# One program per engine for feed-forward and experts, with a first table for four expert pieces

## The reference, cut to what matters

```python
gate_logits = x_flat @ gate_w.T
topk_vals, topk_idx = jax.lax.top_k(gate_logits, K)
topk_w = jax.nn.softmax(topk_vals, axis=-1)
comb = comb.at[jnp.arange(T)[:, None], topk_idx].add(topk_w)
for e in range(E):
    h = jax.nn.gelu(x_flat @ w1[e].T + b1[e], approximate=False)
    y = h @ w2[e].T + b2[e]
    out = out + comb[:, e:e + 1] * y
```

## Time and profile before

| what | value |
|---|---|
| median of 3 runs | 1071.52 us (1066.3 to 1072.51) |
| profiled execution, its own time | 1073.44 us |
| its span in the trace | 1071.7 us |
| PE busy in the span | 948.8 us (89%) |
| DVE, ACT, POOL busy | 671.1, 729.5, 540.6 us |
| granted TensorE clock, mean | 0.947 of full |

### The profile page before, as it was taken

The page is one execution under the profiler, slowest core; times in us unless marked ns, Lnnn a source line. Parts: engine busy times, 40 slices in busy tenths (PEclk is TensorE's granted clock), DMA queues, the critical chain, the costliest instruction groups (busy, mean ns, idle before and its releaser), DMA issues. The chain is left out here.

```text
span 1071.7 us, 20795 instructions
## 1 busy us (share of the span) xinstructions
PE 948.8 (89%) x6750; PEld 574.4 (54%) x6750; DVE 671.1 (63%) x1979; ACT 729.5 (68%) x917; POOL 540.6 (50%) x480
## 2 busy tenths in 40 slices
PE   2788999999999999999999988898930999999993
PEld 1355444444444444444444444464820898989873
DVE  6668587887878878788787745644643343434421
ACT  3536799899998999989999945653310645455551
POOL 6647486767667676676657972000453123232321
PEclk9899899999999999999999999998955999999997
DMA  9596766645366453664575464910542123232323
GB/s 282 157 268 179 203 213 224 232 156 179 120 220 240 160 180 118 218 242 142 167 265 194 143 217 141 421 63 21 207 173 73 40 44 62 43 59 40 47 38 94
DMA packets 74298, 168.43 MB, mean 157 GB/s; under 512 B 13586, under 2 KB 42386, under 8 KB 68242
## 3 DMA queue, kind: packets, MB, share of 16 engines
q1 hardware_dynamic: 50354, 97.99, 28.1%
q0 software_dynamic: 19984, 67.93, 21.0%
q10 hardware_dynamic: 3856, 1.19, 0.5%
HBM read 120.84 MB, written 61.96 MB: 171 GB/s over the span
## 5 line engine op out<-in xcount | busy, mean ns | idle before, releaser
L973 DVE CUSTOM_DVE_ANT_0 masked<-ps,maskA 128x512 f32<-128x512 f32 x512 | 346.5, 688 | 106.7 <-PE ps L1575 104.4
L1398 ACT ACTIVATE masked<-masked,negmax 128x2048 f32<-128x2048 f32 x128 | 256.7, 2005 | 33.8 <-DVE negmax L979 31.0
L1484 ACT ACTIVATE weights<-ps 128x1024 f32<-128x1024 f32 x256 | 248.7, 1010 | 32.3 <-PE ps L1600 31.9
L1575 PE MATMUL ps<-ks,qs 96*128 96x512 f32 x512 | 257.7, 537 | 13.2 <-DVE piecemax L973 9.0
L1598 PE MATMUL ps<-qs,ks 98*128 98x512 f32 x512 | 228.1, 505 | 2.4 <-DMA qs<-shift_lo 2.3
L1600 PE MATMUL ps<-maskB,identb 128*128 128x512 bf16 x512 | 202.8, 396 | 0.0
L1575 PEld LDWEIGHTS ps<-ks,qs 96*128 96x128 f32 x512 | 99.5, 194 | 96.7 <-DVE piecemax L973 75.8
L1876 POOL DMA_INDIRECT sum_rows<-y,ids x39 | 60.3, 1547 | 174.7 <-DVE y L1914 163.8
L1612 PE MATMUL ps<-weights,v_all 128*32 128x256 f32 x2048 | 137.7, 386 | 0.9 <-ACT weights L1484 0.9
L725 POOL TENSOR_SCALAR maskB<-adjB 128x1024 bf16<-128x1024 int32 x32 | 116.6, 3642 | 36.3 <-DMA adjB<-in_adjT 33.0
L1896 DVE TENSOR_TENSOR gT<-ffn_w,gT 128x2048 f16<-128x2048 f32 (+1 forms) x23 | 45.2, 1967 | 129.3 <-ACT gT L1953 129.3
(11 more groups left out here) (209 smaller groups left out, 1152.9 us busy)
## 6 DMA issues: line engine op xcount, KB each, us to landing
expert_rows<-pad_rows POOLq DMA_DIRECT2D x73, 272.0 KB, 5.9
split_weights<-whl POOLq DMA_DIRECT2D x36, 512.0 KB, 3.4
adjA<-in_adj SPq DMA_DIRECT2D x16, 1024.0 KB, 7.3
adjB<-in_adjT SPq DMA_DIRECT2D x32, 512.0 KB, 5.8
wall<-split_weights SPq DMA_DIRECT2D x16, 1024.0 KB, 15.8
wch<-in_w1T POOLq DMA_DIRECT2D x14, 512.0 KB, 5.9
wch<-in_w2T POOLq DMA_DIRECT2D x14, 512.0 KB, 6.2
xr<-expert_rows SPq DMA_DIRECT2D x16, 272.0 KB, 2.8
```

Source lines behind the costliest of these rows:

```text
L973: dve.tensor_tensor_reduce(masked[:, a % 2, k * 512:(k + 1) * 512], ps[:, u % 2, :], maskA[:, a, k * 512:(k + 1) * 512], 1.0, NO_EDGE, ALU ...
L1398: act.activation(masked[:, a % 2, :], masked[:, a % 2, :], ACT.Exp, bias=negmax[:, h % 2, a:a + 1], accum_out=rowsum[:, h % 4, a:a + 1]).t ...
L1484: act.activation(weights[:, j % 4, :, :], ps[:, 2 + 2 * (j % 2):4 + 2 * (j % 2), :], ACT.Exp).then_inc(weights_ready, 1)
L1575: pe.matmul(ps[:, u % 2, :], qs[0:KR, h % 4, a * P:(a + 1) * P], ks[0:KR, h, k * 512:(k + 1) * 512], start=True, stop=True)\
```

## The change

The two blocks become one, so that each engine runs from feed-forward into experts in its own order. The routing of block b is moved up beside the feed-forward of later blocks: on PE `back` is cut into four tiles, and `back(2)` goes ahead of `hidden(3)`. `rows` has three buffers, and PSUM places of the gates and ranks differ by block. The exponential goes from ACT to POOL, as a power of e (`gap_power`). `scatter(2)` is cut in two around `row_factors(1, 3)`.

There are two tables. `early_table` uses the counts after three blocks: 1536 rows make 3072 choices, and at least four pairs of 256 rows are then full, whatever the draw. It gives the first four pieces, which are loaded after `scatter(0)` to `scatter(2)`. `final_table` gives the other 19 (12 wide, 7 narrow), loaded after `scatter(3)`. `ranks(3)` stands in the middle of `first_half(0)`, `send(3)` and `scatter(3)` behind it. The number of pieces and of expert matmuls is the same. The biases `b2b` are loaded after the rows of pieces 0 and 1. The two 256-column halves of a piece's result share PSUM bank 4, where banks 4 and 5 held one each.

```diff
+        EARLY = 4
+        LATER = SLOTS - EARLY
...
+        rows_of = [at(f"rows{i}", [P, TPB, ROW], F32, where)
+                   for i, where in enumerate((M_WCH, M_WCH + 4352, M_ADJA))]
+        rows_of.append(rows_of[1])
         xb = at("xb", [P, 2, TPB, D], F32, M_WCH + 8704)
...
+                def load_rows(j):
+                    w = wide(j) * P
+                    if j == 0:
+                        sp.wait_ge(scattered[0], 32 * TOPK * TPB)
+                        sp.wait_ge(scattered[1], 16 * TOPK * TPB)
+                        sp.wait_ge(table_ready, 2)
+                    elif j == EARLY:
+                        sp.wait_ge(scattered[1], 32 * TOPK * TPB)
+                        sp.wait_ge(table_ready, 4)
+                    sp.dma_start(xr[:, j % 2, 0:wide(j), :], expert_rows[bass.ds(first_row(sp, j), w), :]
+                                 .rearrange("(a p) d -> p a d", p=P)).then_inc(row_in[j % 2], 16)
...
                 store_x1(3)
-                for b in range(2):
-                    sp.wait_ge(x1_out[b], 32)
-                sp.wait_ge(c_in, 32)
+                for j in range(2):
+                    load_rows(j)
+                sp.dma_start(b2b[:, :, :], b2.rearrange("e d -> (e d)").partition_broadcast(P)).then_inc(c_in, 16)
+                for j in range(2, SLOTS):
+                    sp.wait_ge(xT_ready, j - 1)
+                    sp.wait_ge(meta_ready, j - 1)
+                    load_rows(j)
...
+                def gap_power(b):
+                    pool.wait_ge(gap_ready, b + 1)
+                    pool.tensor_tensor(gap[:, 1, :], euler[:, :], gap[:, 0, :], ALU.pow).then_inc(gap_exp, 1)
...
+                def scatter(b, tiles=range(TPB)):
...
+                gap_power(0)
+                row_factors(1, 1)
                 pool.wait_ge(prefilled, 16 * (E * REGION // PR + 1))
                 scatter(0)
                 row_factors(1, 2)
+                gap_power(1)
                 scatter(1)
+                gap_power(2)
+                scatter(2, range(0, 2))
                 row_factors(1, 3)
-                scatter(2)
+                scatter(2, range(2, TPB))
+                gap_power(3)
+                for q in range(2):
+                    for a in range(2):
+                        to = T + (2 * q + a) * (P // 2)
+                        pool.dma_start(sum_rows[to:to + P // 2, :], pad_rows[0:P // 2, 0:D])\
+                            .then_inc(added[q][a], 16)
                 scatter(3)
-                for q in range(2):
-                    pool.wait_ge(scattered[q], 16 * TOPK * NT // 2)
+                for b in range(2):
+                    pool.wait_ge(x1_out[b], 32)
+                for j in range(SLOTS):
...
+                def early_table():
+                    dve.wait_ge(rank_read, 4)
+                    dve.wait_ge(c3_ready, 16)
+                    then(dve.tensor_tensor(taken[:, 0, :], place[:, :], region0[:, :], ALU.subtract))
...
+                def final_table():
...
+                                               group[:, i, E - reach:E + G2 - reach], ALU.add))
+                    ends = group[:, 4, E:E + G2]
+                    then(dve.tensor_tensor(base[:, G2 + 1:2 * G2 + 1], base[:, 1:G2 + 1], base[:, 0:G2], ALU.subtract))
+
...
                 ffn_sum(1, 0)
+                new_x(1, (0, 1))
+                new_stats(1, (0, 1))
+                choose_first(0)
+                dve.wait_ge(rank_read, 1)
+                choose_second(0)
...
+                new_x(1, (2, 3))
+                new_stats(1, (2, 3))
+                new_moments(1)
...
                 split_turned(3)
+                send(0)
+                ffn_sum(2, 0)
+                new_x(2, (0, 1))
+                new_stats(2, (0, 1))
+                ffn_sum(2, 1)
+                new_x(2, (2, 3))
                 for f in range(FC):
                     split_hidden(3, f)
-                    if f in (0, 2):
-                        new_x(1, (f, f + 1))
+                    if f == 0:
+                        new_stats(2, (2, 3))
+                        new_moments(2)
                     elif f == 1:
...
-                new_stats(2, range(TPB))
-                new_moments(2)
-                choose_first(1)
-                choose_second(1)
+                        choose_first(1)
+                    elif f == 2:
+                        choose_second(1)
+                    elif f == 4:
+                        send(1)
+                choose_first(2)
+                choose_second(2)
                 ffn_sum(3, 0)
                 new_x(3, (0, 1))
-                send(1)
+                new_stats(3, (0, 1))
+                send(2)
                 ffn_sum(3, 1)
                 new_x(3, (2, 3))
-                new_stats(3, range(TPB))
+                new_stats(3, (2, 3))
                 new_moments(3)
-                choose_first(2)
-                choose_second(2)
-                send(2)
+                early_table()
                 choose_first(3)
                 choose_second(3)
+                dve.memset(credit4[:, 0:1], 0.0).then_inc(y_ready, 1)
+                for j in range(2):
+                    low_rows(j)
+                    keep_meta(j)
                 send(3)
...
+                low_hidden(0)
+                final_table()
+                dve.wait_ge(c_in, 32)
+                for j in range(SLOTS):
+                    if j + 2 < SLOTS:
+                        low_rows(j + 2)
+                    if j + 1 < SLOTS:
+                        low_hidden(j + 1)
+                    weigh(j)
+                    if j + 2 < SLOTS:
+                        keep_meta(j + 2)
...
                 high_turned(3)
+                normalise_x(1)
+                copy_xnT(1)
                 for f in range(FC):
                     hidden_high(3, f)
-                gap_exponential(0)
-                normalise_x(1)
-                copy_xnT(1)
-                gap_exponential(1)
-                normalise_x(2)
+                    if f == 6:
+                        normalise_x(2)
                 copy_xnT(2)
                 normalise_x(3)
-                gap_exponential(2)
                 copy_xnT(3)
-                gap_exponential(3)
+                for j in range(2):
+                    high_rows(j)
+                act.wait_ge(c_in, 32)
...
+                        if j == 0 and m == HC // 2:
+                            ranks(3)
...
+                                mm = pe.matmul(ps[:, 4, a * D:(a + 1) * D], gT4[j % 2][:, g, m, a * P:(a + 1) * P],
...
                 turn_h2(3)
+                for a in range(TPB):
+                    back(2, a)
+                    if a == 0:
+                        pe.wait_ge(c3_ready, 12)
+                        ranks(0)
+                    elif a == 1:
+                        turn_xn(1)
+                    elif a == 2:
+                        gates(1)
                 for f in range(FC):
                     hidden(3, f)
                     if f == 4:
-                        pe.wait_ge(c3_ready, 12)
-                        ranks(0)
-                back(2, 0)
-                turn_xn(1)
-                back(2, 1)
-                gates(1)
-                back(3, 0)
-                ranks(1)
-                back(3, 1)
+                        ranks(1)
                 turn_xn(2)
-                gates(2)
-                ranks(2)
+                for a in range(TPB):
+                    back(3, a)
+                    if a == 0:
+                        gates(2)
+                    elif a == 2:
+                        ranks(2)
                 turn_xn(3)
                 gates(3)
...
                 pe.wait_ge(experts_in, 32 * E)
+                pe.wait_ge(table_ready, 2)
                 this = expert(pe, 0)
                 first_half(0, this)
...
                     if j + 1 < SLOTS:
+                        if j + 1 == EARLY:
+                            pe.wait_ge(table_ready, 4)
                         following = expert(pe, j + 1)
                         first_half(j + 1, following)
```

More of the change, by code:

```diff
@@ L383, in graph_attention_and_experts, with wide, tiles_to, adds_to @@
         table_ready = sem("table_ready")
+        row_in = [sem("row_in0"), sem("row_in1")]
+        xT_ready = sem("xT_ready")
+        xT_high = sem("xT_high")
+        xT_split = sem("xT_split")
+        mid_ready = sem("mid_ready")
+        mid_gelu = sem("mid_gelu")
+        mid_high = sem("mid_high")
+        mid_split = sem("mid_split")
+        end_ready = sem("end_ready")
+        y_step = sem("y_step")
+        y_ready = sem("y_ready")
+        meta_ready = sem("meta_ready")
+        added = [[sem(f"added{q}{a}") for a in range(2)] for q in range(2)]
+        out_done = sem("out_done")
+        MB = HC // 2
+        def wide(j):
+            return 2 if j < NPAIR else 1
+        def tiles_to(j):
+            return sum(wide(i) for i in range(j))
+        def adds_to(j, q, a):
```

(26 more changed lines are left out.)

513 lines of the change are left out of this document (239 added, 274 removed).

## The result

| | before | after |
|---|---|---|
| median | 1071.83 us (4 runs, 1066.3 to 1072.51) | 1042.9 us (4 runs, 1042.26 to 1045.9) |
| ratio of the runs | 1 | 0.9771, 95% interval 0.9744 to 0.9798 |
| profiled execution, its span | 1073.44, 1071.7 us | 1042.73, 1041.0 us |
| start of `back(1)` in the span | 715.94 | 714.68 |
| from there to the first expert matmul | 114.31 | 82.23 |

Faster by 2.3%, 24.5 us by the ratio (21.6 to 27.4). So I compare **offsets from the start of `back(1)`**: 29.4 less to the end, 32.1 less to the first expert matmul. (PE's timeline of before has its start at 830.25; the chain in the earlier trace rows, which counts it from the end of the transposes, at 830.39.)

The account below looks back on a forecast made before the run. PE fills the experts, so an earlier start comes off the end one for one: 31.3 earlier - 0.4 ranks(3) - 2.8 table wait - 1.3 clock = 26.8 saved; 1071.52 - 26.8 = 1044.7 us, range 1037 to 1054.

Parts of the forecast that it names:

- end of the slots of block 2: DVE, from ffn_sum to the targets of block 2: 4.6 us with two statistics between, ending at 776.9.
- last issue of `scatter(2)` ends: POOL: four issues 5.1, factors of block 3 1.3, four more issues and their lead 5.2, ending at 789.4.
- row load: SP: scatter landed at 791.9, 1.0 to read the table, then 6.2 from row load to first matmul.
- first expert matmul: PE starts the experts at 799.1 on the profiled clock, 31.3 us earlier than before.
- wait behind the final table: PE in the experts waits 2.8 us for low_rows(2), which DVE takes in order behind final_table.
- clock behind that wait: If the clock falls in the table's wait, the halves behind lose up to 2.6 us; 1.3 taken.
- 2.0 behind `ranks(1)`: PE in the feed-forward: clock expected to fall in the wait at ranks(1); 2.0 us added (0 to 2.8).
- (4): Rival: the block's end is not removed but the engines' own loop start; the 6.5 stay, 1051.2; chance 0.04.
- (2): Rival: landing of scatter(2) takes 6.8 because weights and x rows are queued; 4.3 later, 1049.0; chance 0.12.
- (3): Rival: DVE keeps POOL from its descriptors; eight issues of scatter(2) wait at most 0.7 each, 5.6 later, 1050.3; chance 0.05.
- (5): Rival: slower than before; the wait behind the final table drops the clock through the experts; with five pieces 1097; chance 0.03.
- The exponential costed at nothing: Exponential moved from ACT to a POOL power of about 1.04 us, beside DVE's work; costed at nothing.

Follow-up runs that it names:

- choose1_early: Changed kernel with choose_first(1) and choose_second(1) moved on DVE ahead of ffn_sum(2, 1); median 1038.39 us, ratio to before 0.9730.
- long_subtracts: Changed kernel plus three unused 128x2048 DVE subtractions, both operands in SBUF, beside scatter(2); one run, 334.81 us from back(1) to the end (changed kernel 326.32).
- late_routing: Changed kernel with the routing set back to the order of the kernel before, early pieces kept; ratio to before 0.9849.
- joined: Kernel before with its two blocks made one and nothing else, SP waiting for all scatters and the table; ratio to before 0.9942.
- exp_act: Changed kernel with the exponential back on ACT; one run, 330.38 us from back(1) to the end (changed kernel 326.32).
- psum_subtracts: Changed kernel plus six unused 128x1024 DVE subtractions with the f32 operand from PSUM; one run, 327.28 us from back(1) to the end (changed kernel 326.32).
- scatter2_whole: Changed kernel with scatter(2) in one piece and row_factors(1, 3) behind it; one run, 334.02 us from back(1) to the end (changed kernel 326.32).

## Why the prediction was right

It gave 1044.7 (1037 to 1054); the median is 1042.9. Step by step, as offsets from `back(1)`:

| step | forecast | measured |
|---|---|---|
| end of the slots of block 2 | 61.0 | 60.6 |
| last issue of `scatter(2)` ends | 73.5 | 73.5 |
| row load | 77.0 | 76.0 |
| first expert matmul | 83.2 | 82.2 |
| wait behind the final table | 2.8 | 2.93 |
| clock behind that wait | 1.3 | 0.0 |
| `ranks(3)` | 0.4 | 0.3 |

- **The start of the experts** was right to 1.0, and the whole of this 1.0 is the landing: I counted 2.5 from the end of the last issue, and it runs from its start (787.18 and 2.44).
- **The 26.8 saved** were 29.4 between the two profiles. Besides that 1.0, the clock's 1.3 didn't come, and the first half lost less than in the kernel before, where its 48 matmuls took 7.17 against 6.30 in the chain here (3.65 and 2.65). The medians are 28.9 apart; the ratio says 24.5, with an interval that holds 26.8. Closer than some 3 us the forecast can't be judged, since the runs of before alone spread over 6.
- **The clock.** The terms of 2.0 behind `ranks(1)` (5.73 against 4.04 without the fall in choose1_early, so 1.7; 2.8 in four other kernels with the same order) and 1.3 (0 to 2.6) were rightly given as ranges. That the second came out at 0.0 is luck: in three kernels the clock fell there. One half-microsecond window of the changed kernel behind `ranks(1)`, and one at the end of the table's wait:

```profile
754.50:755.00 0.50, 0.50 (x3) 0.19 (x2) 0.20 (x2) 0.00 (x0) 0.38 (x1) 0.50 0.20 68
```

```profile
817.00:817.50 0.50, 0.00 (x0) 0.00 (x0) 0.48 (x1) 0.00 (x0) 0.00 (x0) 1.00 0.00 0
```

Behind `ranks(1)` the clock had fallen to 1.2 GHz (0.50); at the end of the table's wait it was still at 2.4 (1.00), and the half behind took 5.41, as at full clock.
- **The rivals.** The block's end was removed (4). The landing did not take 6.8 (2). DVE did not keep POOL from `scatter(2)` (3), but only because no long instruction with two SBUF operands stands beside it: my two rows of 0.97 were beside table steps of 0.54 or none, which show nothing of it, and the argument from them was wrong. The mechanism is there. Its price in long_subtracts, 4.5, is near my 5.6 by chance: three issues were longer by 1.0 to 1.9, where I had summed eight by 0.7. In the changed kernel it struck `scatter(3)`, which has time. The clock did not stay low in the experts (5).
- **The exponential costed at nothing:** the power on POOL costs nothing, but leaving ACT's loads where the exponential would stand costs some 2 us of PE's waits, and in the old order the exponential of block 2 came 3.1 later than the power (late_routing); so the edit has a worth that the forecast didn't name. The sum was not touched, since its walk had the power in it.

What the forecast had not seen is that the parts need each other. Against joined, earlier routing without early pieces saves 3.9, early pieces without earlier routing 12.6 (each with the power, the buffers and the PSUM places), and all together 22.8.

## What to carry to other kernels

An early start needs all of its parts: find which producer the first consumer waits for, and move that one forward; bringing another forward gives little until it does. After such a move, walk each engine's queue past the new start and look for a long group that stands ahead of something short that is wanted, as the table stood ahead of `low_rows(2)`; cut it where the engine idles. And compare profiles from a common instruction, not from the span's start, when the stretch ahead drifts by more than the effect.

## What the runs showed of the hardware

- **A long DVE instruction with two SBUF operands holds up POOL's indirect DMA issues.** In all ten kernels with `send(3)` inside the experts one issue of `scatter(3)` lasted 2.79 to 2.99 where `low_hidden(0)` (2.29, both operands in SBUF) ran beside it. The Trainium skill, "SBUF — State Buffer", section "Who interferes with whom", says that an instruction with two SBUF inputs contends with a GpSimd instruction that reads SBUF; these runs agree (1.95 to 2.90 against 0.97 to 1.05 from PSUM).
- **A wait of 2.9 does not decide the clock.** Ahead of the third first half PE waited 2.90 to 2.94 in seven kernels; behind it the half took 5.41 in four (after, exp_act, psum_subtracts, late_routing) and 6.89, 7.08 and 8.34 in three (choose1_early, scatter2_whole, long_subtracts). The three are those whose first 24 matmuls of the experts took longest (4.84 to 5.30, in the four others 3.69 to 4.64); seven runs are too few to make a rule of it, and what tells them apart stays open. A wait taken away did not always win its fall back, which then showed at the next wait.
